# The last unit of a graph-and-experts kernel stored in two halves by the sync queue, one Gelu issued ahead, and the last batch of exponentials taken as powers on GpSimd

## The chip, the cores and the metric

The kernel runs on one core of a Trainium2 chip. The time is the device time of one execution in microseconds (us). PE is TensorE, DVE is VectorE, ACT is ScalarE, POOL is GpSimd, SP is the sync engine; SP, ACT and POOL can each issue transfers.

## The reference, cut to what matters

Two layers on `x` of 8 x 2048 x 128: a normalised graph product, then a mixture of eight experts of which each token uses two.

```python
x = x + relu(einsum('nm,bmo->bno', L_norm, layernorm(x) @ W))      # graph stage
tokens = layernorm(x)                                             # 16384 tokens of 128
logits = tokens @ router_w.T
probs = softmax(logits)
rw, re = top_k(probs, 2);  rw = rw / rw.sum(-1)                   # gates of a token
out = tokens
for e in range(8):
    h = gelu(tokens @ w1[e] + b1[e])                              # the exact Gelu
    out = out + combine[:, e:e + 1] * (h @ w2[e] + b2[e])
x = x + out
```

## The kernel before, in words

The work is cut into `U = 32` units of 512 token columns (128 features by 4 x 128 tokens). Three stages follow each other in the program of every engine: setup (the adjacency matrix is summed and scaled), graph (units in one order), experts (units 0 to 31). Every product is made in three parts, high by high, high by low and low by high, to keep float32 accuracy.

Nothing schedules the work but the order of the code: each engine runs its own list, and waits on semaphores.

**The expert stage.** A unit has eight steps, one for each expert `e`; step `t = 8u + e` is counted from the start of the stage. In a step PE makes the three products of `up_product` (L1356 to L1358), ACT takes `Gelu` of the result (L1408, `act_h`), DVE multiplies by the gates (L1446, `gated`), ACT rounds that to the high part (L1415, `g_hi`), DVE subtracts for the low part (L1451, `g_lo`), and PE, three steps later, makes the three products of `down_product` (L1369, L1370, L1372). On DVE the order in a step is `gated` of this step, then `g_lo` of the step before. Once a unit, ACT copies the sum out (L1420, `o_t`), PE turns it with four transposes (L1378), DVE adds the residual (L1459, `fin`, at `e == 6` of the next unit) and POOL stores it (L1339). `fin` has two buffers, so `finish(u)` waits until the store of unit `u - 2` has landed. The first `KNOWN = 6` units are written out, the others run in a hardware loop of two units; SP loads the inputs of a unit two units ahead.

**The tail of the graph stage inside the expert stage.** The last graph unit's layernorm, its router product and the routing of the last batch of four units (batch 7) are not done when the experts start. Their pieces stand in tables, keyed by the step after which they run: `tail_tensor`, `tail_scalar`, `tail_vector`. Each piece is a handful of small instructions on DVE. Of batch 7, `largest` (step 17) makes `shifted`, the logits less their maximum; `exps` (ACT, step 19) makes `expo`; `add_picked` (step 31) waits for it; `weigh`, `split_gate` and `turn_gates` follow (steps 35, 39, 43), and the gates are stored behind the store of unit `KNOWN - 1`. Those gates are first read for unit 16.

ACT evaluates one loaded table of functions at a time; `Exp` and `Gelu` need different ones, and the program loads a table (ACT_TABLE_LOAD) ahead of the first instruction that needs it.

**The end.** After the loop of units PE makes the last three `down_product`s, ACT copies, PE turns, DVE adds and POOL stores unit 31, each as one instruction group over 512 columns; then POOL waits for both `stored` semaphores.

**Powers on POOL.** POOL has one other use of `ALU.pow`: reciprocal roots of variances, on tiles of 128 x 3 to 128 x 8 (L296, L576, L1020).

Of the kernel before, what the change touches and what calls it, by code (L numbers as in the profile page):

```python
# [4 lines left out]
FP32 = mybir.dt.float32  # L5
FP32R = mybir.dt.float32r
ALU = mybir.AluOpType
ACT = mybir.ActivationFunctionType
AX = mybir.AxisListType

P = 128
# [17 lines left out]
def gnn_moe_kernel(nc, x, adj, gnn_w, router_w, w1, b1, w2, b2, out):  # L29
    B, N, D = x.shape  # L30
    E = router_w.shape[0]
    MB = N // P
    CW = 512
    Q = CW // P
    U = 2 * MB
    v = Plan()
# [15 lines left out]
    with ctx:  # L52
# [91 lines left out]
        v.var_eps = sb("var_eps", [P, Q], FP32, at)  # L144
        v.rstd = sb("rstd", [P, Q], FP32, at)
        T = v.T = 4 * Q
        v.logits = sb("logits", [P, T, E], FP32, at)
# [621 lines left out]
def graph_stage(nc, sem, v):  # L769
# [17 lines left out]
    z_lo_done = sem("z_lo_done")  # L787
    router_zeroed = sem("router_zeroed")
    router_hi = sem("router_hi")
    router_lo = sem("router_lo")  # L790
# [175 lines left out]
    def scalar(act):  # L966
# [27 lines left out]
        for u in range(U):  # L994
            ahead = u + 1 < MB
            ks = jobs(u)
            if u:
                evict(u - 1)
            if ahead and u:
                st.high_direct(act, u + 1)  # L1000
            for g in range(4):
                if ks and g < 2:
                    pr.copy_x(act, ks[g])
                if ks and g >= 2:
                    pr.high(act, ks[g - 2])
                if u and ahead and g < st.n_groups(u + 1):
                    st.high_group(act, u + 1, g)
            if u:
                copy_z(u - 1)
            if u >= 5 and u % 4 == 1:  # L1010
                exps((u - 5) // 4)
            if u == MB + 5:
                v.weights_high(act)
        evict(U - 1)
        v.tail_scalar = {10: [(copy_z, U - 1)], 13: [(store_last, U - 1)], 19: [(exps, 7)]}

    def gpsimd(pool):
# [14 lines left out]
        pool.wait_ge(v.summed, v.all_groups)  # L1032
        pool.memset(v.router[:, :, :].bitcast(FP32), 0.0).then_inc(router_zeroed, 1)
        for u in range(U):
            if u:
# [14 lines left out]
    def vector(dve):  # L1050
# [122 lines left out]
        for u in range(U):  # L1173
# [19 lines left out]
            for k in jobs(u + 1):  # L1193
                pr.statistics(dve, k)
        mid(U - 1)
        v.tail_vector = {11: [(z_low, U - 1)], 16: [(turn_logits, 7)], 17: [(largest, 7, 0)], 20: [(first_of, 7, 0)],
                         23: [(largest, 7, 1)], 27: [(first_of, 7, 1)], 31: [(add_picked, 7)], 35: [(weigh, 7)],
                         39: [(split_gate, 7)], 43: [(turn_gates, 7)]}

# [11 lines left out]
def expert_stage(nc, sem, v):  # L1211
# [7 lines left out]

    KNOWN = 6  # L1220

# [18 lines left out]
    fin_done = sem("fin_done")  # L1240
    stored = [sem(f"stored{i}") for i in range(2)]

    def load_weights(sp):
# [78 lines left out]
    def sync(sp):  # L1322
# [6 lines left out]
        with sp.Fori(MB // 2, MB) as h:  # L1329
            for s in range(2):  # L1330
                load_unit(sp, h, s, 2 * h + s)

    def gpsimd(pool):
        def store(h, s, u):

            pool.wait_ge(fin_done, u + 1)
            half, n = (0, u) if isinstance(u, int) else (u // MB, u & (MB - 1))
            rows = v.out_units[bass.ds(half, 1), bass.ds(n, 1)]
            pool.dma_start(rows.rearrange("a c p q f -> p (a c q) f"),  # L1339
                           v.fin[s][:, :].rearrange("p (q f) -> p q f", f=P)).then_inc(stored[s], 16)  # L1340
            if isinstance(u, int) and u == KNOWN - 1:
                v.store_gates(pool, U // 4 - 1)

        over_units(pool, store)
        for s in range(2):
            pool.wait_ge(stored[s], 16 * (U // 2))

    def tensor(pe):
# [50 lines left out]
        for e in range(E - LAG, E):  # L1399
            down_product(1, U - 1, e)  # L1400
        turn_out(U - 1)

    def scalar(act):
# [32 lines left out]
        high(U - 1, E - 1)  # L1436
        copy_out(U - 1, 1)

    def vector(dve):
# [35 lines left out]
        low(U - 1, E - 1)  # L1475
        finish(U - 1, 1)

# [23 lines left out]
```

## Time and profile before

| what | value |
|---|---|
| median of 3 runs | 886.82 us (885.3 to 887.14) |
| profiled execution | 886.36 us, span of the trace 884.6 us |
| PE busy | 845.1 us (96% of the span) |
| DVE busy | 639.1 us (72%) |
| ACT busy | 478.5 us (54%) |
| POOL busy | 301.0 us (34%) |
| granted TensorE clock, mean | 0.984 of full |

The span runs from the first to the last instruction; the profiled execution's own time is 1.8 us longer. Busy shares are means over three stages of different make-up, so the stretches around the change are read on their own: the start of the expert stage near 497 us, its first six units to about 580 us, and the last 10 us.

### The profile page before, as it was taken

What the parts mean: (1) busy time and instruction counts of PE and PEld (TensorE: products, weight loads), DVE (VectorE), ACT (ScalarE), POOL (GpSimd) and SP (SyncE); (2) the same over time, 40 slices, a digit from 0 to 9 for tenths busy, and PEclk for the clock granted to TensorE, in tenths of its full rate; (3) what the DMA queues carried; (4) which work ended last, traced back from release to release, by engine and by line L of the source; (5) the groups of instructions that cost most, each with busy time, mean ns of one, the idle gap of its engine ahead of it and who ended that gap; (6) DMA issues with size and microseconds to landing.
All of it is one profiled execution on the core that took longest, in us unless ns stands there. A gap on an engine that the chain in (4) does not pass through costs nothing.

```text
span 884.6 us, 14390 instructions
## 1 busy us (share of the span) xinstructions
PE 845.1 (96%) x4098; PEld 703.2 (80%) x4098; DVE 639.1 (72%) x1557; ACT 478.5 (54%) x872; POOL 301.0 (34%) x311
## 2 busy tenths in 40 slices
PE   3688999999999999999999999999999999999996
PEld 3687788888888888888888777888888888888884
DVE  3678644578898644343425589999999999999995
ACT  2687423224333210111111588888888888888885
POOL 1893253574757444555444610010000000000001
PEclk9996999999999999999999999999999999999999
DMA  9994376686765257977778765677777777777771
GB/s 281 322 313 143 123 273 251 226 286 246 261 227 189 83 198 272 322 287 275 258 267 329 298 247 198 261 280 285 289 282 270 259 273 270 269 288 272 273 289 48
DMA packets 93006, 222.98 MB, mean 252 GB/s; under 512 B 8888, under 2 KB 59600, under 8 KB 81056
## 3 DMA queue, kind: packets, MB, share of 16 engines
q1 hardware_dynamic: 87760, 212.96, 68.0%
q0 software_dynamic: 2688, 8.59, 2.5%
q10 hardware_dynamic: 2512, 0.86, 0.4%
q8 instruction: 23, 0.38, 0.2%
q14 instruction: 23, 0.19, 0.1%
HBM read 157.89 MB, written 64.49 MB: 251 GB/s over the span
## 4 chain that ended last, share of the span: by engine, by line
PE 88%; DVE 5%; ACT 3%; issue 2%; DMA 1%; ACTq 0%; DVEq 0%; POOL 0%; POOLq 0%
PE bank L956 13%; PE bank L958 13%; PE bank L957 13%; PE bank L1372 6%; PE bank L1356 6%; PE bank L1358 6%; PE bank L1357 6%; PE bank L1369 6%; PE bank L1370 6%; PE bank L342 3%; PE bank L893 2%; PE bank L1378 2%; PE bank L323 1%; PE bank L446 1%; ACT s_tri L605 1%
## 5 line engine op out<-in xcount | busy, mean ns | idle before, releaser
L1408 ACT ACTIVATE act_h<-bank,b_sb 128x512 f32<-128x512 f32 x256 | 176.6, 690 | 46.8 <-PE bank L1358 43.4
L1446 DVE TENSOR_TENSOR gated<-c_all,act_h 128x512 f32<-128x512 f32 x256 | 177.6, 694 | 28.6 <-ACT act_h L1408 20.9
L1451 DVE TENSOR_TENSOR g_lo<-gated,g_hi 128x512 fp32r<-128x512 f32 x256 | 175.6, 686 | 0.2
L1415 ACT ACTIVATE g_hi<-gated 128x512 fp32r<-128x512 f32 x256 | 159.3, 622 | 4.9 <-DVE gated L1446 4.9
L1339 POOL DMA_DIRECT2D out<-fin x32 | 24.3, 760 | 343.3 <-DVE fin L1459 332.1
L1025 POOL TENSOR_SCALAR z<-x,mv,rstd 128x128 f32<-128x128 f32 x128 | 106.6, 846 | 3.4
L956 PE MATMUL bank<-y_hi,stage 128*128 128x512 f32 x256 | 105.6, 413 | 1.6 <-DVE y_lo L732 0.9
L1356 PE MATMUL bank<-z_e,w_hi 128*128 128x512 f32 x256 | 103.4, 404 | 2.6 <-ACT act_h L1408 2.5
L978 ACT ACTIVATE z_hl<-bank 128x512 fp32r<-128x512 f32 x32 | 19.1, 598 | 155.3 <-PE bank L893 155.3
L1372 PE MATMUL bank<-g_lo,w_hi 128*128 128x512 f32 x256 | 101.1, 395 | 0.9 <-DVE g_lo L1451 0.7
L956 PE MATMUL bank<-y,stage 128*128 128x512 f32 x256 | 101.2, 395 | 0.0
L958 PE MATMUL bank<-y_hi,stage 128*128 128x512 f32 x256 | 101.1, 395 | 0.0
L957 PE MATMUL bank<-y_lo,stage 128*128 128x512 f32 x256 | 100.6, 393 | 0.0
L1369 PE MATMUL bank<-g_hi,w_lo 128*128 128x512 f32 x256 | 100.2, 391 | 0.0
L1358 PE MATMUL bank<-z_e,w_lo 128*128 128x512 f32 x256 | 100.2, 391 | 0.0
L1357 PE MATMUL bank<-z_e,w_hi 128*128 128x512 f32 x256 | 100.1, 391 | 0.0
L1370 PE MATMUL bank<-g_hi,w_hi 128*128 128x512 f32 x256 | 99.9, 390 | 0.0
L958 PE MATMUL bank<-y,stage 128*128 128x512 f32 x256 | 99.9, 390 | 0.0
L957 PE MATMUL bank<-y,stage 128*128 128x512 f32 x256 | 99.7, 389 | 0.0
L1020 POOL TENSOR_TENSOR rstd<-var_eps,neg_half 128x4 f32<-128x4 f32 x32 | 37.8, 1180 | 154.4 <-DVE var_eps L1064 154.4
L1068 DVE TENSOR_TENSOR z_hl<-bank,z_hl 128x512 fp32r<-128x512 f32 x32 | 22.0, 689 | 78.5 <-ACT z_hl L978 78.5
L1372 PEld LDWEIGHTS bank<-g_lo,w_hi 128*128 128x128 f32 x256 | 48.1, 188 | 14.0 <-DVE g_lo L1451 3.9
(127 smaller groups left out, 1474.8 us busy)
## 6 DMA issues: line engine op xcount, KB each, us to landing
c_all<-c_scratch SPq DMA_DIRECT2D x64, 1024.0 KB, 8.0
s_scratch<-stage SPq DMA_DIRECT2D x14, 2048.0 KB, 8.2
stage<-s_scratch SPq DMA_DIRECT2D x14, 2048.0 KB, 8.0
z_e<-z_scratch SPq DMA_DIRECT2D x32, 512.0 KB, 7.0
z_scratch<-z_hl SPq DMA_DIRECT2D x31, 512.0 KB, 2.7
x_raw<-in_x SPq DMA_DIRECT2D x32, 256.0 KB, 6.7
x_res<-in_x SPq DMA_DIRECT2D x32, 256.0 KB, 7.1
r_e<-res_scratch SPq DMA_DIRECT2D x32, 256.0 KB, 2.7
```

The lines of the kernel that those rows point to most:

```text
L956: pe.matmul(out[:, :], s_hi, y_hi, start=(i == 0), stop=False)
L957: pe.matmul(out[:, :], s_hi, y_lo, start=False, stop=False)
L958: last = pe.matmul(out[:, :], s_lo, y_hi, start=False, stop=(i == MB - 1))
L1356: pe.matmul(ps_h[k][:, :], v.w1_hi[:, e, :], v.z_e[s][:, 0, :], start=True, stop=False)
L1357: pe.matmul(ps_h[k][:, :], v.w1_hi[:, e, :], v.z_e[s][:, 1, :], start=False, stop=False)
L1358: pe.matmul(ps_h[k][:, :], v.w1_lo[:, e, :], v.z_e[s][:, 0, :], start=False, stop=True).then_inc(h_done, 1)
L1369: pe.matmul(ps_o[s][:, :], v.w2_lo[:, e, :], hi[:, :], start=False, stop=False)
L1372: pe.matmul(ps_o[s][:, :], v.w2_hi[:, e, :], lo[:, :], start=False, stop=(e == E - 1)).then_inc(o_done, 1)
L1408: act.activation(v.act_h[e % R][:, :], ps_h[e % 2][:, :], ACT.Gelu, bias=v.b1_sb[:, e:e + 1]).then_inc(gelu_done, 1)
L1415: act.activation(v.g_hi[e % R][:, :], v.gated[e % R][:, :], ACT.Copy).then_inc(hi_done, 1)
L1446: dve.tensor_tensor(out=v.gated[e % R][:, :], in0=v.c_all[s][:, e, :], in1=v.act_h[e % R][:, :], op=ALU.mult).then_inc(gated_done, 1)
L1451: dve.tensor_tensor(out=v.g_lo[e % R][:, :], in0=v.gated[e % R][:, :], in1=v.g_hi[e % R][:, :].bitcast(FP32), op=ALU.subtract).then_inc(lo ...
```

## The change

Four things change.

1. ACT executes a `Gelu` of one column, into a tile nobody reads, ahead of the last `evict` of the graph stage.
2. The exponentials of batch 7 leave ACT. POOL takes them as eight instructions `pow(e, shifted)` of 128 x 16 elements each, between the stores of units 0 and 1. The pieces `add_picked`, `weigh`, `split_gate` and `turn_gates` move from steps 31, 35, 39, 43 to steps 36, 42, 48, 54.
3. `KNOWN` goes from 6 to 8, so eight units are written out, and the gates of batch 7 are stored behind unit 7.
4. Unit 31 is copied, turned, added and stored in two halves of 256 columns, and SP issues the two stores in place of POOL.

```diff
+        act.activation(v.ahead[:, :], v.one_col[:, :], ACT.Gelu)
         evict(U - 1)
-        v.tail_scalar = {10: [(copy_z, U - 1)], 13: [(store_last, U - 1)], 19: [(exps, 7)]}
+        v.tail_scalar = {10: [(copy_z, U - 1)], 13: [(store_last, U - 1)]}
...
+        pool.memset(v.euler[:, :], 2.718281828459045).then_inc(euler_made, 1)
+        def last_exps(batch):
+
+            pool.wait_ge(shift_done, batch + 1)
+            pool.wait_ge(euler_made, 1)
+            for i in range(0, T, 2):
+                last = pool.tensor_tensor(out=v.expo[:, i:i + 2, :].rearrange("p t e -> p (t e)"), in0=v.euler[:, :],
+                                          in1=v.shifted[:, i:i + 2, :].rearrange("p t e -> p (t e)"), op=ALU.pow)
+            last.then_inc(exp_done, 1)
...
-                         23: [(largest, 7, 1)], 27: [(first_of, 7, 1)], 31: [(add_picked, 7)], 35: [(weigh, 7)],
-                         39: [(split_gate, 7)], 43: [(turn_gates, 7)]}
+                         23: [(largest, 7, 1)], 27: [(first_of, 7, 1)], 36: [(add_picked, 7)], 42: [(weigh, 7)],
+                         48: [(split_gate, 7)], 54: [(turn_gates, 7)]}
...
-    KNOWN = 6
+    KNOWN = 8
...
+        for i in range(2):
+            sp.wait_ge(half_done, i + 1)
+            sp.dma_start(v.out_units[1, MB - 1][:, 2 * i:2 * i + 2, :],
+                         v.fin[1][:, i * HW:(i + 1) * HW].rearrange("p (q f) -> p q f", f=P)).then_inc(half_stored[i], 16)
+        for i in range(2):
+            sp.wait_ge(half_stored[i], 16)
...
+            if isinstance(u, int) and u == 0:
+                v.last_exps(U // 4 - 1)
             if isinstance(u, int) and u == KNOWN - 1:
                 v.store_gates(pool, U // 4 - 1)
...
-        copy_out(U - 1, 1)
+        act.wait_ge(o_done, E * U)
+        act.wait_ge(o_turned, U - 1)
+        for i in range(2):
+            act.activation(v.o_t[:, i * HW:(i + 1) * HW], ps_o[1][:, i * HW:(i + 1) * HW],
+                           ACT.Copy).then_inc(half_copied, 1)
...
-        finish(U - 1, 1)
+        dve.wait_ge(r_in[1], 8 * (U - 1) + 8)
+        dve.wait_ge(stored[1], 16 * (U // 2 - 1))
+        for i in range(2):
+            dve.wait_ge(half_turned, i + 1)
+            dve.tensor_tensor(out=v.fin[1][:, i * HW:(i + 1) * HW], in0=ps_half[i][:, 0:HW],
+                              in1=v.r_e[1][:, i * HW:(i + 1) * HW], op=ALU.add).then_inc(half_done, 1)
```

Where the instructions stand on ACT, at the start of the expert stage: before, the table of `Gelu` is loaded behind the last `evict` (L971), directly ahead of the first `Gelu` (L1408).

```order
L971 ACTIVATE x1_122<-bank0,d_out_58 128x512
L978 ACTIVATE z_hl_126<-bank6 128x512
L971 ACTIVATE x1_122<-bank1,d_out_58 128x512
L1408 ACT_TABLE_LOAD
L1408 ACTIVATE act_h0_167<-bank2,b1_sb_56 128x512
```

The same place in the changed kernel, where L974 is the `evict` and L1450 the first `Gelu`:

```order
L974 ACTIVATE x1_122<-bank0,d_out_58 128x512
L981 ACTIVATE z_hl_126<-bank6 128x512
L1018 ACT_TABLE_LOAD
L1018 ACTIVATE ahead_132<-one_col_50 128x1
L974 ACTIVATE x1_122<-bank1,d_out_58 128x512
L1450 ACTIVATE act_h0_169<-bank2,b1_sb_56 128x512
```

The load has moved to the other side of the last `evict`, and no other load stands between it and the end of ACT's list. At step 19 before, two loads and the exponentials (L982) stood between a copy of `o_t` and the next `Gelu`:

```order
L1420 ACTIVATE o_t_162<-bank1 128x512
L982 ACT_TABLE_LOAD
L982 ACTIVATE expo_138<-shifted_137 128x128
L1408 ACT_TABLE_LOAD
L1408 ACTIVATE act_h0_167<-bank2,b1_sb_56 128x512
L1415 ACTIVATE g_hi3_178<-gated3_174 128x512
```

All three rows between the copy and the `Gelu` are gone from this place in the changed kernel. On POOL, the exponentials (L1045) now stand between the store of unit 0 and that of unit 1 (L1368), where before a store followed a store:

```order
L1035 TENSOR_TENSOR res_124<-x1_122,z_123 128x512
L1368 DMA out<-fin0_165 128x4x128
L1045 TENSOR_TENSOR expo_140<-euler_131,shifted_139 128x16 x8
L1368 DMA out<-fin1_166 128x4x128
L1368 DMA out<-fin0_165 128x4x128
```

The stores of units 1 and 2 are issued behind all eight powers. On DVE, `add_picked` (L1134 to L1142 of the changed kernel) now stands after step 36, two steps ahead of `finish` of unit 3 (L1505), whose buffer `fin1` is the one that the store of unit 1 empties:

```order
L1134 TENSOR_TENSOR same_134<-is_1st_136,is_2nd_138 128x128
L1137 TENSOR_REDUCE sum_all_144<-expo_140 128x16
L1139 TENSOR_TENSOR picked_141<-expo_140,same_134 128x128
L1142 TENSOR_REDUCE sum_top_145<-picked_141 128x16
L1492 TENSOR_TENSOR gated1_174<-c_all0_167,act_h1_170 128x512
L1497 TENSOR_TENSOR g_lo0_181<-gated0_173,g_hi0_177 128x512
L1492 TENSOR_TENSOR gated2_175<-c_all0_167,act_h2_171 128x512
L1497 TENSOR_TENSOR g_lo1_182<-gated1_174,g_hi1_178 128x512
L1505 TENSOR_TENSOR fin1_166<-bank5,r_e1_163 128x512
```

Before, the same four instructions stood after step 31, seven steps ahead of that `finish`.

## Rows read from the trace of the kernel before

**Rows 1.** Page, part 4: engines' shares of the chain that ended last.
```profile
PE 88%; DVE 5%; ACT 3%; issue 2%; DMA 1%; ACTq 0%; DVEq 0%; POOL 0%; POOLq 0%
```
**Rows 2.** Chain that ended last, 440 to 620 us: start, length, what.
```profile
514.98 0.44 PE bank L1378 x4
...
528.06 3.06 issue
...
578.83 0.44 PE bank L1378 x4
...
590.41 0.44 PE bank L1378 x4
```
**Rows 3.** Timeline of ACT, 420 to 600 us: start, busy, what, idle before.
```profile
496.47 0.69 ACT L971 ACTIVATE x<-bank,d_out 128x512 f32<-128x512 f32 x1 [2.16 <-PE bank L958]
497.17 1.28 ACT L1408 ACT_TABLE_LOAD   x1
...
527.42 1.28 ACT L982 ACT_TABLE_LOAD   x1
```
**Rows 4.** Timeline of DVE, 494 to 600 us.
```profile
499.27 0.17 DVE L1064 TENSOR_SCALAR var_eps<-mv 128x4 f32<-128x4 f32 x1
499.35 1.29 DVE L1446 TENSOR_TENSOR gated<-c_all,act_h 128x512 f32<-128x512 f32 x2
...
508.96 1.81 DVE L1446 TENSOR_TENSOR gated<-c_all,act_h 128x512 f32<-128x512 f32 x1
...
525.16 0.29 DVE L1095 TENSOR_TENSOR shifted<-logits,top 128x128 f32<-128x128 f32 x1
...
525.57 0.69 DVE L1446 TENSOR_TENSOR gated<-c_all,act_h 128x512 f32<-128x512 f32 x1
...
549.57 0.29 DVE L1118 TENSOR_TENSOR same<-is_1st,is_2nd 128x128 f32<-128x128 f32 x1
...
550.50 0.68 DVE L1446 TENSOR_TENSOR gated<-c_all,act_h 128x512 f32<-128x512 f32 x1
```
**Rows 5.** Groups of POOL by form: xcount, busy us, mean ns, idle before.
```profile
L576 POOL TENSOR_TENSOR d_inv<-deg_safe,neg_half 128x8 f32<-128x8 f32 x1 | 1.7, 1668 | 0.0
```
**Rows 6.** Timeline of POOL, 460 to 600 us.
```profile
488.84 3.13 POOL L1025 TENSOR_SCALAR z<-x,mv,rstd 128x128 f32<-128x128 f32 x4
...
499.52 1.41 POOL L1020 TENSOR_TENSOR rstd<-var_eps,neg_half 128x4 f32<-128x4 f32 x1 [6.18 <-DVE var_eps L1064]
501.03 7.81 POOL L1025 TENSOR_SCALAR z<-x,mv,rstd 128x128 f32<-128x128 f32 x4
508.93 1.29 POOL L1030 TENSOR_TENSOR res<-x,z 128x512 f32<-128x512 f32 x1
```
**Rows 7.** Timeline of all engines, 463.5 to 466.5 us.
```profile
464.08 1.03 POOL L1020 TENSOR_TENSOR rstd<-var_eps,neg_half 128x4 f32<-128x4 f32 x1 [6.18 <-DVE var_eps L1064]
...
464.95 0.29 DVE L1078 TENSOR_TENSOR logits<-gate_parts 128x128 f32<-128x128 f32 x1
```
**Rows 8.** Landing: all 32 POOL stores; DMA issues 530 to 600; SP stores.
```profile
DMA to landing us min/median/max: 2.7/6.7/8.0
...
out<-fin POOLq DMA_DIRECT2D x6, 256.0 KB, 4.1
...
res_scratch<-res SPq DMA_DIRECT2D x31, 256.0 KB, 2.0
```
**Rows 9.** Chain that ended last, 874 to 885 us.
```profile
876.26 0.61 ACT o_t L1420
...
877.60 0.70 DVE fin L1459
...
879.19 0.73 POOL out L1339
```
**Rows 10.** Groups by form, of DVE (100 to 500 us) and of ACT.
```profile
L460 DVE TENSOR_TENSOR stage<-bank,stage 128x256 fp32r<-128x256 f32 x3 | 1.3, 423 | 6.0 <-ACT stage L453 6.0
...
L453 ACT ACTIVATE stage<-bank 128x256 fp32r<-128x256 f32 x4 | 1.5, 382 | 8.2 <-PE bank L446 8.2
```

More of the change, by code:

```diff
@@ L145, in gnn_moe_kernel @@
         v.rstd = sb("rstd", [P, Q], FP32, at)
+        v.euler = sb("euler", [P, 2 * E], FP32, at)
+        v.ahead = sb("ahead", [P, 1], FP32, at)
         T = v.T = 4 * Q
@@ L788, in graph_stage @@
     router_zeroed = sem("router_zeroed")
+    euler_made = sem("euler_made")
     router_hi = sem("router_hi")
@@ L1033, in gpsimd @@
         pool.memset(v.router[:, :, :].bitcast(FP32), 0.0).then_inc(router_zeroed, 1)
+        pool.memset(v.euler[:, :], 2.718281828459045).then_inc(euler_made, 1)
[6 more added lines that the diff above has]
+            last.then_inc(exp_done, 1)
+        v.last_exps = last_exps
         for u in range(U):
@@ L1241, in expert_stage @@
     stored = [sem(f"stored{i}") for i in range(2)]
+    half_copied = sem("half_copied")
+    half_turned = sem("half_turned")
+    half_done = sem("half_done")
+    half_stored = [sem(f"half_stored{i}") for i in range(2)]
+    ps_half = [v.banks[5], v.banks[6]]
+    HW = CW // 2
     def load_weights(sp):
@@ L1336, in store @@
             pool.wait_ge(fin_done, u + 1)
-            half, n = (0, u) if isinstance(u, int) else (u // MB, u & (MB - 1))
+            half, n = (u // MB, u % MB) if isinstance(u, int) else (u // MB, u & (MB - 1))
             rows = v.out_units[bass.ds(half, 1), bass.ds(n, 1)]
@@ L1340, in store @@
                            v.fin[s][:, :].rearrange("p (q f) -> p q f", f=P)).then_inc(stored[s], 16)
+            if isinstance(u, int) and u == 0:
+                v.last_exps(U // 4 - 1)
             if isinstance(u, int) and u == KNOWN - 1:
                 v.store_gates(pool, U // 4 - 1)
-        over_units(pool, store)
+        for u in range(KNOWN):
+            store(u // 2, u % 2, u)
+        with pool.Fori(KNOWN // 2, U // 2 - 1) as h:
+            for s in range(2):
+                store(h, s, 2 * h + s)
+        store(U // 2 - 1, 0, U - 2)
         for s in range(2):
-            pool.wait_ge(stored[s], 16 * (U // 2))
+            pool.wait_ge(stored[s], 16 * (U // 2 - s))
     def tensor(pe):
@@ L1400, in tensor @@
             down_product(1, U - 1, e)
-        turn_out(U - 1)
+        pe.wait_ge(fin_done, U - 1)
+        for i in range(2):
+            pe.wait_ge(half_copied, i + 1)
+            for q in range(2):
+                a = i * HW + q * P
+                last = pe.transpose(ps_half[i][:, q * P:(q + 1) * P], v.o_t[:, a:a + P], v.ident[:, :])
+            last.then_inc(half_turned, 1)
     def scalar(act):
@@ L1475, in vector @@
         low(U - 1, E - 1)
-        finish(U - 1, 1)
+        dve.wait_ge(r_in[1], 8 * (U - 1) + 8)
+        dve.wait_ge(stored[1], 16 * (U // 2 - 1))
+        for i in range(2):
+            dve.wait_ge(half_turned, i + 1)
+            dve.tensor_tensor(out=v.fin[1][:, i * HW:(i + 1) * HW], in0=ps_half[i][:, 0:HW],
+                              in1=v.r_e[1][:, i * HW:(i + 1) * HW], op=ALU.add).then_inc(half_done, 1)
     stage = Plan()
```

## The prediction

> **What bounds the kernel now.** I read the chain that ended last first. PE has 88% of it [rows 1], so a change on another engine is worth only what it takes from the stretches where the chain leaves PE. There are three near this change. At the start of the expert stage it passes through ACT, with a table load of 1.28 us between the last `evict` and the first `Gelu` [rows 3]. In the first units it runs over DVE, with a hole of 3.06 us at 528 us in which nothing runs on it [rows 2]: ACT loads the table of `Exp`, makes the exponentials and loads the table of `Gelu` again. At the end it goes ACT, PE, DVE, POOL, then the landing of the last store [rows 9].
>
> How much the first units lose is read from PE's transposes, one group a unit. An undisturbed unit takes 590.41 - 578.83 = 11.58 us. From 514.98 to 578.83 there are five units, 63.85 us, where 57.9 would do: 5.95 us are lost [rows 2]. Of these 3.06 are the hole; the remaining 2.9 are DVE, which runs without idle time there because the routing pieces come on top of its steps. Two of its large instructions back to back take 1.29 us where one takes 0.69, so they start 0.60 apart [rows 4]; a step is 1.2 us of DVE, a unit with its `fin` about 10.3, and its room is 11.58 - 10.3 = 1.3 us a unit, 0.16 a step.
>
> **The change, part by part.**
>
> *The Gelu ahead: 0.* ACT idles 2.16 us ahead of the last `evict` [rows 3]; load (1.28) and one-column `Gelu` (some 0.2) fit in. The first real `Gelu` then no longer stands behind the load. It could start when PE has its first product, 0.9 us earlier. But DVE has its own work to do there, the statistics of the last graph unit, which end with `var_eps` at 499.27 + 0.17, and the first `gated` follows at once, at 499.35, without idle time [rows 4]. That work hangs on the `evict`, which is not moved. So the load has a second path in its shadow only 0.1 to 0.2 us shorter. I take 0; bounds 0 and -0.9.
>
> *Exp off ACT: -3.1.* The 3.06 us hole goes, if DVE can be shown to have work: its next `gated` would need one `Gelu`, which ACT could start as soon as the copy of `o_t` ended at 527.4, where its first load stands [rows 3]. I take all of the hole.
>
> The Trainium skill ("ScalarE: Activation LUTs", What ACT_TABLE_LOAD costs) gives 1283 ns for a load and about 2.66 us for a switch with its drain. The load agrees with the 1.28 us here, the drain does not show: by the page two switches would be 5.3 us, where the hole with the exponentials inside is 3.06, and the row decides.
>
> *Pieces further apart: -0.2.* The four moved pieces are about 0.9, 0.7, 0.5 and 0.6 us of DVE, 2.8 in sum (`add_picked`, for one, from 549.57 to the next `gated` at 550.50 [rows 4]; the others are guessed from their count of instructions). Four steps apart they meet 4 x 4 x 0.16 = 2.6 us of room, six apart 3.8. They stop costing the 0.2 that they exceed by. The pieces of steps 16 to 27 stay, and with them most of the 2.9.
>
> *The powers on POOL.* No power of 128 x 16 is in the trace. 4 elements take 1.03 us [rows 7] and 8 take 1668 ns [rows 5], 160 ns an element, so 16 take about 2.95 us, and eight of those 23.6. They start when `shifted` is made, at 525.16 + 0.29 = 525.45, so undisturbed they end at 549.1.
>
> They are not undisturbed. In the expert stage nearly every DVE instruction has two inputs in SBUF and DVE has no gap. Four `z` instructions of POOL took 3.13 us in the graph stage and 7.81 between DVE's steps: 0.78 became 1.95 [rows 6]. 1.95 is three DVE instructions of 0.60 and 0.1. I read it so: POOL gets its turn to read only when the DVE instruction that runs and the one queued behind it are over. A power of 2.95 us ends in the fifth DVE instruction after its turn, and gets the next turn after the sixth: 6 x 0.605 = 3.63 us apart. With the first turn at 526.2, the last power ends at 526.2 + 7 x 3.63 + 2.95 = 554.6. Bounds: 549.1 and, with two instructions more for each, 564.
>
> What does DVE feel? Where POOL reads few elements, nothing: a 128 x 128 instruction of DVE with both inputs in SBUF started at 464.95 inside a power and took its 0.29 [rows 7], and behind the power at 499.52 two `gated` took 1.29, their undisturbed time. Where POOL reads much, DVE is held: `gated` at 508.96 took 1.81 against 0.69 behind POOL's 128 x 512 `res` [rows 4, 6]. A power of 16 elements reads 32 values, nearer to the first kind. I take 0.03 us each.
>
> *Who waits for the powers.* DVE went from 525.57 to 549.57, that is 24.0 us, or 20.9 without the hole, to the start of `add_picked` at step 31 [rows 4]. Five steps more are 6.0: it reaches step 36 at 552.5. The powers end at 554.6, so DVE waits 2.1 us, and behind it in its queue all of `gated` and `g_lo`. That is not all: the store of unit 1 is queued on POOL behind the powers, and `finish` of unit 3, step 38, needs it landed. Without a wait `finish` comes at 552.5 + 0.9 + 2.4 = 555.8. The six stores of 530 to 600 us landed a median 4.1 us after issue [rows 8], so this one lands at 554.7 + 4.1 = 558.8. The two waits together are 3.0 us, since the second contains the first. After step 27 DVE has caught up nine steps of 0.16, 1.4 us, less what `add_picked` exceeds its room by: some 0.8 us of the wait are hidden, 2.2 are lost. With a landing of 6.7, the median of all 32 [rows 8], it is 4.8; with the powers at 549.1 it is nothing.
>
> *KNOWN at 8, gates later: 0.* The gates are stored two units (23 us) later; they are read for unit 16, eight units behind unit 8. The extra code is straight-line; bounds 0 and +0.3.
>
> *The end: -2.0.* Before: copy at 876.26, `fin` at 877.60 for 0.70, the issue only at 879.19 (0.9 us behind `fin`), landing 2.7 later, the least of its kind [rows 8, 9]: 881.9. After: a half is copied in 0.38 and added in 0.42 [rows 10]. The second half is copied by 876.9, turned by 877.35 (four transposes took 0.67, two some 0.4), added by 877.8. SP issues it 0.1 us later, and SP's stores of 256 KB land 2.0 us after issue [rows 8]: 879.9. What follows the landing, 2.7 us, stays. Bounds: -1.3, if SP's store lands no quicker than POOL's, and -2.6. The store of unit 30 is issued before that of unit 31 and on another queue; I take it to be down by then.
>
> **Sum**, against the profiled execution of 886.36: 0 - 3.1 - 0.2 + 0.2 (DVE held by reads) + 2.2 - 2.0 = -2.9, 883.5. The median of the runs stands 0.46 above the profiled one, so I add half of that: **883.7**. The rivals are worked out from 886.6, the middle of the two.
>
> **The rivals.**
>
> *A. The powers are hidden.* If POOL gets its turn at the end of the running DVE instruction, a power needs 3.03 us, the last ends near 550.4, `add_picked` waits for nothing and the store lands in time. For it: the power at 499.52 was delayed only 0.38 (1.41 against 1.03), and from step 27 on DVE has small gaps. Against it: four `z` in a row. Time: 886.6 - 3.3 - 2.0 = 881.3. 35%.
>
> *B. The forecast*, two waits of 1 to 4 us in sum, 882.3 to 885. 40%.
>
> *C. The waits eat the gain.* The store of unit 1, issued in a full stretch of loads, takes 6.7 to 8.0 us to land, and the waits reach 5.6 to 7: 886.6 - 3.3 + 5 to 6 - 2.0, so 886.3 to 887.3, no change. It needs the powers to end after 553.5. 14%.
>
> *D. Slower: the powers hold DVE.* If a power keeps DVE from its second input as long as it computes, not only as long as it reads, each holds DVE for up to 2.95 us, eight for 23.6, and there is next to no DVE instruction there that could pass. Then 886.6 - 3.3 - 2.0 + 23 = 904; if it holds DVE for half of that time, 893. It turns the sign from 0.7 us for each power. For it stands the `gated` of 1.81 us; against it the 0.29 us of rows 7 and the two `gated` at 499.35. 8%. The Trainium skill says this ("SBUF — State Buffer", Who interferes with whom): whoever comes first has the shared pair for the whole instruction, and a DVE instruction with two SBUF inputs contends with a GpSimd one that reads SBUF. The trace agrees for 512 elements and does not for 4; no run here shows 16.
>
> *E. Something small I don't see* (code fetch of the longer program): 3%, within or above 0.2%.
>
> **The numbers.** 0.2% of 886.8 is 1.8 us, about what a measurement of this kernel can tell from no change. A and B are faster but for B's upper edge: 0.78. C and part of B and E: 0.13 within. D and the rest: 0.09 slower. The range takes A with an end gain of 2.6 (880.7) and reaches to the lower part of C (886.4); D stands outside.
>
> **What would show it.** Right: no table load behind the last `evict` and none near 528, yet the first `gated` at the same time as before (step one), no 3.06 us hole; eight powers started 3.6 us apart; DVE idle ahead of `sum_all` by about 2 us and ahead of `fin` of unit 3 by about 1; SP's second half issued at about 1.6 us after the last copy starts, landing in 2.0. Wrong: powers 3.0 us apart or less and no idle time on DVE (A), `fin` waiting 3 us or more for a store (C), `gated` instructions of 2 to 4 us between 526 and 555 (D), a first `gated` earlier by half a microsecond (my shadow path).

## The result, and the profile after

| | before | changed |
|---|---|---|
| median | 886.18 us (885.3 to 887.14, 6 runs) | 880.43 us (878.45 to 883.34, 6 runs) |
| profiled execution, its span | 886.36 us, 884.6 us | 878.45 us, 876.3 us |

The ratio is 0.9936 with a 95% interval of 0.992 to 0.9951: the changed kernel is 5.7 us faster, 4.3 to 7.1. The forecast was 883.7, and its range began at 880.7. More was gained than forecast.

The profiled execution of the changed kernel is the fastest of its six, and the two executions differ already ahead of the change: the last `evict` starts at 496.47 us before [rows 3] and at 495.01 after. In the other kernels below it starts between 495.2 and 497.7, whatever was edited, so these 1.46 us are no effect of the change. The changed kernel's profiled execution lies 2.0 us below the median of its kernel, and the early start may be most of that. I therefore compare stretches: from the last `evict` to the last copy of `o_t` (the experts), and from that copy to the end of the span (the end).

| stretch | before | changed | difference | forecast |
|---|---|---|---|---|
| experts | 379.79 | 376.91 | -2.88 | -0.9 |
| end | 8.34 | 4.38 | -3.96 | -2.0 |
| outside the span | 1.76 | 2.15 | +0.39 | 0 |

**The start of the expert stage.** Timeline of ACT, 490 to 501 us, of the changed kernel (start, busy, what, idle time before).

```profile
492.87 1.28 ACT L1018 ACT_TABLE_LOAD   x1
...
495.01 0.69 ACT L974 ACTIVATE x<-bank,d_out 128x512 f32<-128x512 f32 x1 [0.64 <-PE bank L961]
496.15 1.37 ACT L1450 ACTIVATE act_h<-bank,b_sb 128x512 f32<-128x512 f32 x2 [0.44 <-PE bank L1394]
498.63 0.63 ACT L1457 ACTIVATE g_hi<-gated 128x512 fp32r<-128x512 f32 x1 [1.11 <-DVE gated L1492]
```

Timeline of DVE, 497.5 to 499 us.

```profile
497.41 0.38 DVE L1077 BATCH_NORM_AGGREGATE mv<-stats 128x2 f32<-128x6 f32 x4
497.82 0.17 DVE L1080 TENSOR_SCALAR var_eps<-mv 128x4 f32<-128x4 f32 x1
497.90 1.29 DVE L1492 TENSOR_TENSOR gated<-c_all,act_h 128x512 f32<-128x512 f32 x2
```

The load now lies ahead of the `evict`, and ACT still idles 0.64 us there. `Gelu` starts 1.14 us behind the start of the `evict`, yet the first `gated` comes 2.89 us behind it, as against 2.88 before [rows 3, 4]: DVE is at its statistics until `var_eps`. ACT has two `Gelu`s done and then waits 1.11 us for DVE. The shadow path is real, and not shorter than the path through the load: taking the load away moved nothing.

**The powers.** Timeline of POOL, 518 to 580 us, and the tile `expo` (x8 and the shortest, median and longest in ns).

```profile
519.04 0.99 POOL L1368 DMA_DIRECT2D out<-fin  x1 [10.27 <-DVE fin L1505]
524.12 23.97 POOL L1045 TENSOR_TENSOR expo<-euler,shifted 128x16 f32<-128x16 f32 x8 [4.08 <-DVE shifted L1111]
548.04 1.56 POOL L1368 DMA_DIRECT2D out<-fin  x2
```

```profile
L1045 POOL TENSOR_TENSOR expo<-euler,shifted x8: 2898/3020/3155, 524.1 to 545.0; 128x16 f32<-128x16 f32 x8
```

They are 3.0 us apart and not 3.63. Timeline of DVE where the results are read:

```profile
551.73 0.29 DVE L1134 TENSOR_TENSOR same<-is_1st,is_2nd 128x128 f32<-128x128 f32 x1
551.93 0.28 DVE L1137 TENSOR_REDUCE sum_all<-expo 128x16 f32<-128x128 f32 x1
...
555.83 0.69 DVE L1505 TENSOR_TENSOR fin<-bank,r_e 128x512 f32<-128x512 f32 x1 [0.70 <-DMA out<-fin]
```

`sum_all` waits for nothing. `fin` of unit 3 waits 0.70 us for the store of unit 1, issued at 548.04, and the two stores issued there take this long to land:

```profile
DMA to landing us min/median/max: 7.7/7.9/8.2
```

So the second wait exists, and is small. In the other kernels with the eight powers ahead of that store and the same steps, its landing took 7.1, 7.3, 7.5 and 7.7 us (experiments three, five, seven, six), and `fin` waited 0, 0.30, 0.47 and 0.71 us. The wait is as long as the landing is late. The unit that contains it took 11.65, 11.82, 12.04 and 12.28 us there, about 11.6 and the wait.

Chain that ended last, 494 to 600 us, PE's transposes, one row for each unit that is read:

```profile
513.56 0.44 PE bank L1414 x4
...
550.39 0.44 PE bank L1414 x4
...
562.63 0.44 PE bank L1414 x4
...
574.21 0.44 PE bank L1414 x4
...
586.07 0.44 PE bank L1414 x4
```

From 513.56 six units take 72.51 us; before it was 590.41 - 514.98 = 75.43 [rows 2]. That is the 2.9 us. The row at 562.63 is 0.66 late by the unit of 11.58: this is where the wait of `fin` is lost. The unit with the hole, from the timelines of PE, before and then changed:

```profile
527.46 0.66 PE L1378 MATMUL bank<-ident,o_t 128*128 128x128 f32 x4
...
543.03 0.60 PE L1378 MATMUL bank<-ident,o_t 128*128 128x128 f32 x4
```

```profile
526.09 0.66 PE L1414 MATMUL bank<-ident,o_t 128*128 128x128 f32 x4
...
538.64 0.60 PE L1414 MATMUL bank<-ident,o_t 128*128 128x128 f32 x4
```

It took 15.57 us and takes 12.55. These six units are the best yardstick for the middle. Behind them nearly all units of all kernels take 11.57 to 11.63 us. The exception is mainly one unit soon after the start of the hardware loop, which takes 11.6 to 12.9 us from execution to execution; where it takes over 12.2, PE waits 0.4 to 1.0 us for a late load of `z_e`. Neither profiled execution in the table above has that loss, most of those below have some of it.

**The end.** Timeline of all engines, 871.9 to the end, without the rows of PE, and the landing of SP's two stores.

```profile
871.92 0.66 ACT L1482 ACTIVATE o_t<-bank 128x256 f32<-128x256 f32 x2 [1.31 <-PE bank L1408]
...
873.00 0.76 DVE L1526 TENSOR_TENSOR fin<-bank,r_e 128x256 f32<-128x256 f32 x2 [1.66 <-PE bank L1442]
873.45 0.93 SPq L1357 DMA_DIRECT2D out<-fin  x2
```

```profile
DMA to landing us min/median/max: 1.9/1.9/1.9
```

The second store is issued at 873.9, lands at 875.8, and the span ends at 876.3. Only 0.5 us stand behind the landing; before they were 884.6 - (879.19 + 2.7) = 2.7 [rows 8, 9].

### The profile page after: what moved, and what is told of

It is laid out like the page before. It is cut to its first block, busy times and chain, and to the rows that moved or that the text cites. A ratio compares the mean times of both kernels' runs of the same rounds, so it can differ in the third digit from the quotient of the medians.

```text
span 876.3 us, 14318 instructions
## 1 busy us (share of the span) xinstructions
PE 840.2 (96%) x4098; PEld 698.8 (80%) x4098; DVE 638.6 (73%) x1558; ACT 476.6 (54%) x871; POOL 325.3 (37%) x319
## 4 chain that ended last, share of the span: by engine, by line
PE 90%; DVE 3%; ACT 3%; issue 2%; DMA 1%; POOL 1%; DVEq 0%; ACTq 0%; POOLq 0%
PE bank L959 13%; PE bank L961 13%; PE bank L960 13%; PE bank L1408 6%; PE bank L1392 6%; PE bank L1394 6%; PE bank L1405 6%; PE bank L1393 6%; PE bank L1406 6%; PE bank L344 3%; PE bank L448 2%; PE bank L896 2%; PE bank L1414 1%; PE bank L325 1%; ACT s_tri L607 1%
## 5 line engine op out<-in xcount | busy, mean ns | idle before, releaser
L1450 ACT ACTIVATE act_h<-bank,b_sb 128x512 f32<-128x512 f32 x256 | 176.9, 691 | 46.2 <-PE bank L1394 37.3
L1368 POOL DMA_DIRECT2D out<-fin x31 | 23.7, 763 | 308.3 <-DVE fin L1505 308.3
L1408 PE MATMUL bank<-g_lo,w_hi 128*128 128x512 f32 x256 | 100.9, 394 | 1.1 <-DVE g_lo L1497 1.0
L1408 PEld LDWEIGHTS bank<-g_lo,w_hi 128*128 128x128 f32 x256 | 48.0, 188 | 14.6 <-DVE g_lo L1497 4.7
```

The lines of the kernel that those rows point to most:

```text
L1408: pe.matmul(ps_o[s][:, :], v.w2_hi[:, e, :], lo[:, :], start=False, stop=(e == E - 1)).then_inc(o_done, 1)
L1450: act.activation(v.act_h[e % R][:, :], ps_h[e % 2][:, :], ACT.Gelu, bias=v.b1_sb[:, e:e + 1]).then_inc(gelu_done, 1)
```

## The experiments

Twelve kernels, each a small edit of one of the two. The first four do one part of the change alone, on the kernel before.

**One: the Gelu ahead.**

```diff
+        act.activation(v.ahead[:, :], v.one_col[:, :], ACT.Gelu)
         evict(U - 1)
```

> The kernel before with the one-column Gelu ahead of the last evict and nothing else. Theory S (a shadow path: the first gated of the expert stage waits for DVE's statistics, not for the table): no gain, the first gated still starts 2.9 us after the last evict starts, 0 to -0.2 us. Rival T (the table load was the chain): the first gated follows up to 0.9 us earlier and the time falls by 0.9 us.

885.58 us, ratio 0.9997 (0.9983 to 1.001). Timelines of ACT and of DVE:

```profile
493.05 1.28 ACT L1015 ACT_TABLE_LOAD   x1
...
495.19 0.69 ACT L972 ACTIVATE x<-bank,d_out 128x512 f32<-128x512 f32 x1 [0.64 <-PE bank L959]
```

```profile
498.00 0.17 DVE L1066 TENSOR_SCALAR var_eps<-mv 128x4 f32<-128x4 f32 x1
498.08 1.29 DVE L1448 TENSOR_TENSOR gated<-c_all,act_h 128x512 f32<-128x512 f32 x2
```

The first `gated` is 2.89 us behind the `evict` once more. The edit is worth nothing by itself.

**Two: the end alone**, everything else as before.

```diff
-        copy_out(U - 1, 1)
...
+        for i in range(2):
+            act.activation(v.o_t[:, i * HW:(i + 1) * HW], ps_o[1][:, i * HW:(i + 1) * HW],
+                           ACT.Copy).then_inc(half_copied, 1)
...
+        for i in range(2):
+            sp.wait_ge(half_stored[i], 16)
```

> The kernel before with only the end changed (halves, stored by SP). From the start of the last copy of o_t to the end of the span the kernel before took 8.34 us and the changed one 4.38. Theory N (all of it is the new end): 4.4 us here too, the time falls by 3.5 to 4.2 us. Rival M (part of it comes from the eight unrolled units or from POOL being free earlier): 5 to 6.4 us, the time falls by 2 to 3 us.

882.97 us, ratio 0.9965 (0.9954 to 0.9977): 3.1 us gained (2.0 to 4.1), the end 4.34 us. The end is theory N's; the time gained lies a little under its 3.5 to 4.2, with an interval that reaches into it. The profiled execution lost 1.3 us in the unit with the late load of `z_e`. The end alone gains about as much as was forecast for the whole change.

**Three: the powers alone**, with the later steps and `KNOWN` at 8.

```diff
-        v.tail_scalar = {10: [(copy_z, U - 1)], 13: [(store_last, U - 1)], 19: [(exps, 7)]}
+        v.tail_scalar = {10: [(copy_z, U - 1)], 13: [(store_last, U - 1)]}
...
+            if isinstance(u, int) and u == 0:
+                v.last_exps(U // 4 - 1)
```

> The kernel before with the powers on POOL, the pieces six steps apart and eight units written out; no Gelu ahead and the old end. Between the last evict and the last copy of o_t the changed kernel took 376.9 us against 379.8. Theory P (all of that is the powers and steps): 376.9 here, the time falls by 2.9 us, with the 0.7 us wait of the fin of unit 3 for the store of unit 1. Rival T (the Gelu ahead gave 0.9 of it): 377.8, the time falls by 2.0 us.

883.71 us, ratio 0.9978 (0.9963 to 0.9994): 1.9 us gained (0.5 to 3.3). Six units take 586.42 - 514.46 = 71.96 us, 3.5 less than before. From `evict` to copy it is 377.2 us, nearer to theory P's 376.9 than to T's 377.8, though a unit with a late `z_e` cost 0.8 in it. The wait of `fin` that theory P expected does not come: the store of unit 1 lands after 7.1 us, in time.

**Four: the later steps and `KNOWN` at 8 alone.**

```diff
-31: [(add_picked, 7)], 35: [(weigh, 7)], 39: [(split_gate, 7)], 43: [(turn_gates, 7)]}
+36: [(add_picked, 7)], 42: [(weigh, 7)], 48: [(split_gate, 7)], 54: [(turn_gates, 7)]}
-    KNOWN = 6
+    KNOWN = 8
```

> The kernel before with the pieces moved to steps 36, 42, 48, 54 and eight units written out; the exponentials stay on ACT at step 19. Theory P (the table loads are worth their 3.06 us hole, spacing 0.2): time falls by 0.2 to 0.5 us, the hole stays. Rival W (the pieces behind step 27 were what DVE was late by): falls by 1 us or more, since the pieces find more room, and most of the 2.9 us of the middle is theirs.

885.62 us, ratio 0.9999 (0.9984 to 1.0014). Timeline of DVE:

```profile
529.85 0.69 DVE L1446 TENSOR_TENSOR gated<-c_all,act_h 128x512 f32<-128x512 f32 x1 [3.06 <-issue]
```

The hole stands, so it belongs to ACT's exponentials and loads, and goes with them only. The six units take 588.54 - 513.66 = 74.88 us, 0.24 less than in experiment one (588.85 - 513.73 = 75.12), the -0.2 of the forecast. The kernels of experiments two and twelve, with the old steps too, take 75.1 as well; the 75.43 of the kernel before contains one unit that took 0.3 longer in its execution. Another 0.4 is given back where the trace doesn't reach: the profiled executions of the four kernels with `KNOWN` at 6 (before, one, two, twelve) are 1.64 to 1.76 us longer than their spans, those of all ten with `KNOWN` at 8 are 2.01 to 2.16 longer. The eight-unit program costs about 0.4 us outside the span (0.3 by experiment four, which has it without the powers and the new end); why, the profile doesn't show.

**Five to seven: what the end is made of.** All three are edits of the changed kernel. In five unit 31 is copied, turned and added whole, and SP stores it whole:

```diff
+        sp.wait_ge(fin_done, U)
+        sp.dma_start(v.out_units[1, MB - 1], v.fin[1][:, :].rearrange("p (q f) -> p q f", f=P)).then_inc(half_stored[0], 16)
+        sp.wait_ge(half_stored[0], 16)
```

In six the block with the halves' two stores and their waits moves from SP's list to POOL's, ahead of POOL's other last waits. In seven SP stores the halves and POOL waits for them:

```diff
-        for i in range(2):
-            sp.wait_ge(half_stored[i], 16)
...
         for s in range(2):
             pool.wait_ge(stored[s], 16 * (U // 2 - s))
+        for i in range(2):
+            pool.wait_ge(half_stored[i], 16)
```

> The changed kernel, but unit 31 is copied, turned, added and stored whole, by SP. End stretch (start of the last o_t copy to the end of the span): 8.34 us before, 4.38 in the changed kernel. Theory Q (who issues and waits is what counts, halves are worth 0.5): 4.9 us. Rival H (the halves carry most of it): 6.5 us or more.

> The changed kernel, but POOL issues the two half stores and waits for them. Theory Q: the end stretch is near 7.8 us, since POOL's issue is later, lands 0.7 later and what follows the landing is 2.7 us again. Rival H: 5 us.

> The changed kernel, SP issues the half stores, but POOL and not SP waits for them at the end. The stretch behind the landing is 2.7 us before and about 0.5 in the changed kernel. Theory Q1 (POOL needs 2 us to end its program behind its last wait): end stretch 6.4 us. Theory Q2 (what lasts is the end of a transfer issued by POOL): 4.4 us as in the changed kernel.

880.17, 882.53 and 883.99 us, one execution each; the ends of the spans are what is read. Timelines of all engines, of five, six and seven, the last store (the copies start at 873.34, 873.08 and 875.54).

```profile
875.40 0.42 SPq L1356 DMA_DIRECT2D out<-fin  x1
```

```profile
874.88 1.42 POOL L1377 DMA_DIRECT2D out<-fin  x2 [2.94 <-DVE fin L1526]
```

```profile
877.07 0.94 SPq L1357 DMA_DIRECT2D out<-fin  x2
```

**Twelve: the wait alone.** The kernel before, with POOL's whole store, but its last two waits on SP.

```diff
+        for s in range(2):
+            sp.wait_ge(stored[s], 16 * (U // 2))
...
-        for s in range(2):
-            pool.wait_ge(stored[s], 16 * (U // 2))
```

> The kernel before, unit 31 still stored whole by POOL, but the two last waits on the stores stand at the end of SP's list and not of POOL's. Before, copy start to the end of the span was 8.34 us, with 2.7 us behind the landing. Theory one (POOL needs about 2 us to get from its last wait to its end, SP some 0.5; POOL's waiting in place of SP's made the changed end 6.36 in place of 4.38): copy to end 6.3 to 6.4, time 884.2 against 886.2, ratio 0.9977. Rival one (what is slow is POOL having issued a transfer as the last thing, whoever waits): 8.3, no change. Rival two (part is the landing itself, which the last wait sees later for a POOL store): 7.0 to 8.0.

884.83 us, ratio 0.9987 (0.9975 to 1.0). Timeline of all engines at the end (the span ends at 883.6):

```profile
876.56 0.60 ACT L1420 ACTIVATE o_t<-bank 128x512 f32<-128x512 f32 x1 [1.32 <-PE bank L1372]
...
879.48 0.75 POOL L1341 DMA_DIRECT2D out<-fin  x1 [3.53 <-DVE fin L1459]
```

The six ends, in us from the start of the last copy:

| kernel | stored by, waited for by | last issue | + landing | + behind it | end |
|---|---|---|---|---|---|
| before | POOL whole, POOL | 2.93 | 2.7 | 2.7 | 8.34 |
| twelve | POOL whole, SP | 2.92 | 2.7 | 1.4 | 7.04 |
| six | POOL halves, POOL | 2.5 | 2.2 | 2.6 | 7.32 |
| seven | SP halves, POOL | 2.0 | 1.9 | 2.5 | 6.36 |
| five | SP whole, SP | 2.06 | 2.3 | 0.4 | 4.76 |
| changed | SP halves, SP | 2.0 | 1.9 | 0.5 | 4.38 |

With the last wait on POOL 2.5 to 2.7 us stand behind the landing, whoever stores; with wait and store on SP it is 0.4 to 0.5. Seven against changed is the wait alone, 1.98 us. Five against changed is the cut alone, 0.38 us: most of the gain is SP and not the halves. Five and seven came out as theories Q (4.9) and Q1 (6.4) had it; six was expected near 7.8 and took 7.32, since POOL's halves were issued and landed sooner than the whole.

Twelve missed theory one (6.3 to 6.4) and rival one (8.3); its 7.04 lies at the lower edge of rival two (7.0 to 8.0: the last wait sees the landing of a POOL store later). With the wait on SP but the last issue on POOL 1.4 us remain. Either POOL, having issued a store of its own so late, ends last, or rival two holds; six and seven, where POOL waits for POOL's and for SP's stores, differ by only 0.1 behind the landing, which speaks against rival two. No run separates the two any further, so what the 1.4 us are stays open.

**Eight: one power for the eight.**

```diff
-            for i in range(0, T, 2):
-                last = pool.tensor_tensor(out=v.expo[:, i:i + 2, :].rearrange("p t e -> p (t e)"), in0=v.euler[:, :],
+            last = pool.tensor_tensor(out=v.expo[:, :, :].rearrange("p t e -> p (t e)"), in0=v.euler[:, :],
```

> The changed kernel with the eight powers of 16 elements as one power of 128 elements (euler is 128 wide). By 160 ns an element it lasts about 21 us. Theory F (POOL reads far ahead of what it computes, so DVE is held only while values are read): no DVE instruction between 524 and 545 us takes more than 0.3 us longer than 0.69, time as the changed kernel. Theory L (POOL keeps its reads until the last element is taken up, and only the first few dozen values fit ahead): one gated or g_lo of 10 us or more, and the time rises by about that.

879.76 us, one execution. Timeline of POOL:

```profile
525.66 20.81 POOL L1044 TENSOR_TENSOR expo<-euler,shifted 128x128 f32<-128x128 f32 x1 [4.09 <-DVE shifted L1110]
546.44 1.55 POOL L1367 DMA_DIRECT2D out<-fin  x2
```

128 elements take 20.8 us, where eight of 16 took 24.0: seven instructions more cost 3.2 us, 0.45 each, and an element 159 ns. The store of unit 1 comes 20.8 us behind the start of the powers, 3.1 earlier than in the changed kernel, and `fin` of unit 3 waits for nothing.

What DVE feels is read from its `gated` during the powers, 525 to 548 us (shortest, median and longest in ns). First this kernel, then the changed one, and for the changed one also the `gated` that runs when its first power starts, which lies ahead of 525.

```profile
L1491 DVE TENSOR_TENSOR gated<-c_all,act_h x15: 676/684/975, 525.7 to 546.9; 128x512 f32<-128x512 f32 x15
```

```profile
L1492 DVE TENSOR_TENSOR gated<-c_all,act_h x16: 676/686/709, 525.4 to 547.7; 128x512 f32<-128x512 f32 x16
```

```profile
524.14 0.74 DVE L1492 TENSOR_TENSOR gated<-c_all,act_h 128x512 f32<-128x512 f32 x1
```

One `gated`, the one that runs when the power starts, is 0.29 us longer than the median; the other fourteen take their usual time, in the middle of a power of 20.8 us. With 64 elements (kernel ten, below) the longest was 0.16 over the median. With 16 it is 0.05 at the first power and 0.02 at the others. So a power does not hold DVE as long as it computes; what it costs grows with its elements, some 2 to 3 ns for each, which fits a hold while it reads, though no run shows the reading itself.

**Nine: the old steps, with the powers.** The changed kernel with `add_picked` early enough that it must wait.

```diff
-36: [(add_picked, 7)], 42: [(weigh, 7)], 48: [(split_gate, 7)], 54: [(turn_gates, 7)]}
+31: [(add_picked, 7)], 35: [(weigh, 7)], 39: [(split_gate, 7)], 43: [(turn_gates, 7)]}
```

> The changed kernel with the last routing pieces back at steps 31, 35, 39 and 43. It prices a wait of DVE for the powers, which the prediction took from the stretch after step 27 as partly hidden. In the changed kernel the powers end at 548.1 us and step 36 is reached at 551.7, so step 31 is reached five steps of 1.2 earlier, at about 545.7, and DVE waits some 2.4 to 2.9 us ahead of sum_all. The wait ahead of fin of unit 3 (0.70) then goes, since fin comes later than the landing. Theory one (DVE has 0.16 us of room a step and has regained some 0.8 us by then): 1.6 to 2.1 us of the wait are lost and 0.7 given back, so the time from the last evict to the last copy goes from 376.9 to about 378.0, and the whole to about 881.3. Theory two (every wait of DVE is lost in full): 378.6 to 379.1. Theory three (the slack hides it all): 376.3 to 376.9, no change.

884.01 us, ratio 0.998 (0.9967 to 0.9993): 3.6 us slower than the changed kernel. None of the three theories holds. Timelines of DVE and of PE, then windows (length, busy us of PE, PEld, DVE, ACT and POOL, the granted clock, the transfers' share and rate):

```profile
546.76 0.30 DVE L1134 TENSOR_TENSOR same<-is_1st,is_2nd 128x128 f32<-128x128 f32 x1
549.63 0.29 DVE L1137 TENSOR_REDUCE sum_all<-expo 128x16 f32<-128x128 f32 x1 [2.57 <-POOL expo L1045]
```

```profile
548.39 0.39 PE L1406 MATMUL bank<-g_hi,w_hi 128*128 128x512 f32 x1
551.69 0.67 PE L1408 MATMUL bank<-g_lo,w_hi 128*128 128x512 f32 x1 [2.91 <-DVE g_lo L1497]
552.15 0.63 PE L1392 MATMUL bank<-z_e,w_hi 128*128 128x512 f32 x1
...
555.14 0.46 PE L1392 MATMUL bank<-z_e,w_hi 128*128 128x512 f32 x1
555.44 0.40 PE L1393 MATMUL bank<-z_e,w_hi 128*128 128x512 f32 x1
555.67 0.40 PE L1394 MATMUL bank<-z_e,w_lo 128*128 128x512 f32 x1
```

```profile
546.00:549.00 3.00, 2.78 (x13) 1.96 (x11) 1.06 (x3) 1.59 (x3) 3.00 (x2) 1.00 0.75 251
549.00:551.00 2.00, 0.00 (x0) 0.00 (x0) 1.34 (x5) 0.00 (x0) 2.00 (x3) 1.00 0.98 371
551.00:552.00 1.00, 0.31 (x1) 0.31 (x2) 1.00 (x3) 0.93 (x2) 0.10 (x1) 0.93 1.11 410
552.00:554.00 2.00, 2.00 (x6) 1.53 (x6) 2.00 (x4) 1.23 (x3) 0.00 (x0) 0.50 1.04 305
554.00:555.00 1.00, 1.00 (x4) 0.81 (x3) 0.65 (x2) 1.00 (x3) 0.00 (x0) 0.50 0.94 328
```

DVE waits 2.57 us, PE runs dry for 2.91, and when it resumes the granted clock stands at 0.50, that is 1.2 GHz in place of 2.4. From 551.69 to 555.14 eight matmuls start in 3.45 us, where eight of 0.23 take 1.8. So 1.6 us come on top of the 2.9: the transposes of that unit stand 16.4 us behind the last (540.19 and 556.59), 4.8 more than 11.6. In that unit the wait of DVE costs nearly twice itself, and nothing is hidden. Over the six units it is 4.0 us more than in the changed kernel, since `fin` of unit 3 no longer waits and the unit that the late pieces fall into is faster; the medians, 3.6 apart, agree with that.

The same run says what the powers' pace depends on. DVE is idle from 547.06 on, for all but the first half microsecond of the last power, the eighth (546.5 to 549.6). It takes 3062 ns; the eighth takes 3063 in experiment three and 3064 in the changed kernel, where DVE is at full work. The other seven agree in these three kernels within 11 ns too (2.93, 3.12, 3.15, 3.06, 2.96, 2.89, 2.98), as the row of nine's powers shows beside that of the changed kernel. Behind their start at least, DVE's work has no effect on them that could be seen; none of these powers started beside an idle DVE.

```profile
L1045 POOL TENSOR_TENSOR expo<-euler,shifted x8: 2892/3022/3148, 525.6 to 546.5; 128x16 f32<-128x16 f32 x8
```

**Ten and eleven: the store of unit 1 among the powers.** Ten takes two powers of 128 x 64, eleven eight of 128 x 16; both store unit 1 behind the first half.

```diff
-            if isinstance(u, int) and u == 0:
-                v.last_exps(U // 4 - 1)
+            if isinstance(u, int) and u < 2:
+                v.last_exps(U // 4 - 1, u)
```

> The changed kernel with the powers as two instructions of 128x64, the store of unit 1 between them. From the single power of 128x128 (20.8 us) and eight of 128x16 (24.0 us), a power costs some 2.6 us per 16 elements and 0.4 us of its own, so each takes about 10.6 us and they end near 547.5 with the store's issue between. Unit 1 is stored near 537 and has landed by 546, nine us before fin of unit 3. Theory one: both the 0.70 us wait ahead of fin goes and add_picked waits for nothing; the time from the last evict to the last copy is 376.3 to 376.6 (the single power had 376.65 and no wait), 0.3 to 0.6 less than the changed kernel, 880.0 against 880.4. Rival one: a power of 64 elements reads 128 values and holds DVE for that, seen as gated instructions of over 1 us next to the start of each power: time as the changed kernel. Rival two: the transfer's issue waits for the end of a power and DVE is slower during the issue (POOL writes descriptors): no gain.

> The changed kernel with its eight powers cut in two groups of four, the store of unit 1 between the groups. It changes only where that store stands. The powers end 1 us later, near 549, and step 36 is reached near 551.7, so add_picked still waits for nothing. Theory one: the 0.70 us wait ahead of fin of unit 3 goes and with it 0.66 us of the late transposes near 562.6; evict to copy 376.3. Rival: those 0.7 us had been regained anyway in the following units by the room of 0.16 us a step, and the time stays at 376.9.

879.9 us, ratio 0.9938 (0.992 to 0.9957), and 879.95 us, ratio 0.9928 (0.9907 to 0.9948). Neither can be told from the changed kernel's 0.9936 in time. In the chain that ended last of eleven:

```profile
552.89 0.44 PE bank L1415 x4
...
564.49 0.43 PE bank L1415 x4
```

11.60 us where the changed kernel has 12.24. The wait of `fin` is gone in both, as theory one said, and was worth 0.64 us; ten lost 0.8 again to a late load of `z_e` in its profiled execution, and 0.7 more in the unit after the start of the loop, so its 377.8 us from `evict` to copy miss the 376.3 to 376.6 that were expected. Eleven has 376.7, with 0.5 lost in that unit. The gain shows in the units and not in the times.

The powers behind a store are slower: the fifth of eleven, issued directly behind the store of unit 1, took 3.40 us where it took 2.97 in the changed kernel, and the second of ten took 11.0 where its first took 10.6. `gated` took up to 0.75 us in eleven, at the start of its sixth power, and up to 0.81 in ten, at the start of its second.

## Why the forecast was wrong, point by point

- **The Gelu ahead, 0: right**, and by the reason given. 2.88 and 2.89 us from `evict` to `gated` in before, after and experiment one.
- **Exp off ACT, -3.1: right.** The unit with the hole takes 3.02 us less (15.57 and 12.55). Experiment four shows that the later steps alone leave the hole.
- **Pieces further apart, -0.2: right** (0.24). The four guessed pieces add up to 2.7 and not 2.8, which would have made it -0.1; the agreement is within what was guessed.
- **DVE held by reads, +0.2: right** (0.05 us at the first power, about 0.02 at each of the others). Rival D is out, for 16 elements and for 128. The Trainium skill's rule ("SBUF — State Buffer", Who interferes with whom), that whoever comes first has the shared pair for its whole instruction, is not what these runs show of powers: one of 20.8 us made one `gated`, with two inputs in SBUF, 0.29 us longer.
- **Waits for the powers, +2.2: the first step that failed.** The forecast said "POOL gets its turn to read only when the DVE instruction that runs and the one queued behind it are over", and so 3.63 us a power, an end at 554.6 and waits of 3.0 us. Measured: 3.0 us a power, no dependence on DVE, an end at 548.1 (with `shifted` 1.3 us earlier than in the kernel before), no wait of `sum_all` and one of 0.70 us ahead of `fin`, 0.66 lost. The rule had been read off the four `z` that took 7.81 us; it doesn't carry over to powers. The number next to it, 160 ns an element and 2.95 us a power, was the right one, and with it the undisturbed end of 549.1 that the forecast gave as its lower bound. A second term of the same sum erred the other way: the store of unit 1 was taken to land after 4.1 us, the median of its window, and took 7.7, nearer to the 6.7 of all 32 that Rival C went by. With powers of 3.0 us and a landing of 4.1 there would have been no wait at all; with powers of 3.63 us and 7.7 the loss would have been larger than forecast. That only 0.66 us were lost is the pace's doing. Rival A named this outcome, though its mechanism, a turn at the end of each DVE instruction, isn't borne out either.
- **The pricing of a wait failed too**, without entering the result. The forecast let 0.8 of 3.0 us be hidden; experiment nine lost 4.8 in the unit for a wait of 2.57: PE stood still for 2.91, and 1.6 more went because the clock of TensorE fell. By this run a wait of 3.0 us, the size forecast, would have cost some 4 to 5 us and not 2.2, an estimate.
- **`KNOWN` at 8, 0: 0.4 us too low.** It is lost outside the span.
- **The end, -2.0: the second step that failed, at the sentence "What follows the landing, 2.7 us, stays".** The forecast gave no reason for it. It is 0.5 us, 2.2 less, since SP has the last wait (experiment seven, with the wait on POOL, has 2.5). The rest of the term held: issue at 2.0 us behind the copy (1.6 forecast), landing in 1.9 (2.0 forecast).

Put together: -2.9 forecast, less 2.0 for the experts and 2.0 for the end, plus 0.4 outside the span, is -6.5, inside the measured 4.3 to 7.1. Of the 2.0 for the experts 1.5 are the waits, 0.66 lost in place of 2.2, and 0.3 is the slow unit in the execution before. The two parts alone, experiments two and three, gained 3.1 and 1.9, whose sum of 5.0 agrees too. Both failed steps lay in one direction, and the range, which allowed the end at most 2.6, allowed only one of them at a time. The range's lower edge, Rival A with the larger end gain, was 880.7; the 2.2 us behind the landing had no bound of their own in it.

## What to carry to other kernels

Time between the last landing and the end of the span is a term with its own price, and depends on which engine waits last: look at it, and let SP issue and wait for the last store before cutting the store in pieces. Long element-wise powers on POOL ran at a steady pace and cost DVE next to nothing here (0.2 us over eight), so they can take exponentials off ACT when that saves two table loads, if they end before the reader's step and no store that someone needs is queued behind them. A slowdown that was read off one kind of POOL instruction should not be priced into another; and a short wait that lets PE run dry is to be priced with the slower clock after it.

## What the runs showed of the hardware

- POOL's `pow` took about 159 ns for each element of a partition and 0.45 us an instruction: 20.8 us for 128, 10.6 and 11.0 for 64, 2.9 to 3.15 for 16 (3.40 directly behind a store). The time of one depends on its place in the batch and repeats within 11 ns in three kernels. That it hangs on the values is a guess; no run changed them.
- A last wait on POOL was followed by 2.5 to 2.7 us to the end of the span, one on SP by 0.4 to 0.5 for SP's own store and 1.4 for POOL's.
- A granted clock of 0.50 after PE had been idle for 2.91 us lasted some 3.5 us. In the kernel before, PE's clock fell behind the hole at 528 us as well (0.50 from 533 to 536 us); in experiment one, with the same hole, it stayed at 1.00, and the unit took 15.57 and 15.58 us. There DVE was the bound and the clock cost nothing.
